# A graph layer with attention and routed experts: the last group of the middle stage in another order

## The reference

```python
deg = maximum(segment_sum(ones, dst, 6250), 1)
xn = layernorm(x)                                   # 6250 x 512
x = x + gnn(xn, src, dst, deg) + attention(xn)      # 100000 edges, 8 heads, linear attention
t = layernorm(x)
shared = sum over 2 of  gelu(t @ sw1.T + sb1) @ sw2.T + sb2
probs = softmax(t @ gate_w.T + gate_b)              # 8 experts, the two best of each row
routed = sum over the two best e of  probs[e] * (gelu(t @ rw1[e].T + rb1[e]) @ rw2[e].T + rb2[e])
out = x + shared + routed
```

## Time and profile before

| what | value |
|---|---|
| median of 3 runs | 2157.23 us (2155.22 to 2158.01) |
| the profiled execution | 2157.89 us |
| its span | 2156.3 us |
| its granted TensorE clock | 0.979 of full |
| TensorE busy over the span | 2012.7 us (93%) |
| VectorE busy | 1524.0 us (71%) |
| ScalarE busy | 1070.1 us (50%) |
| GpSimd busy | 1274.1 us (59%) |
| the stretch of the change | 1472.8 to 1519.8 us |

### The profile page before, as it was taken

One profiled execution on the slowest core, in us unless ns is written; L12 is line 12 of the kernel. 1 busy time (PEld: TensorE's weight loads), 2 busy tenths in 40 slices (PEclk: granted clock), 3 DMA queues, 4 the chain that ended last, 5 costly groups with the idle time before them and its releaser, 6 DMA issues. The chain is left out here.

```text
span 2156.3 us, 47156 instructions
## 1 busy us (share of the span) xinstructions
PE 2012.7 (93%) x12724; PEld 1356.5 (63%) x12725; DVE 1524.0 (71%) x3774; ACT 1070.1 (50%) x2102; POOL 1274.1 (59%) x1360
## 2 busy tenths in 40 slices
PE   5999997999999999999999999995799999889998
PEld 2555554666666666666666666663577777667776
DVE  7888885668887787877888787886344444356666
ACT  3555774645546565565645555452344444323332
POOL 3666776777777777777777777760233333153442
PEclk9999998999999999999999999997799999999999
DMA  8855646788888888888888888874455555567765
GB/s 294 271 163 171 247 163 174 226 257 265 261 266 270 259 255 259 264 256 258 256 260 268 252 258 259 262 236 166 146 166 175 170 167 170 165 218 259 256 241 203
DMA packets 187677, 492.47 MB, mean 228 GB/s; under 512 B 41357, under 2 KB 54157, under 8 KB 185833
## 3 DMA queue, kind: packets, MB, share of 16 engines
q0 software_dynamic: 91920, 306.84, 47.0%
q1 hardware_dynamic: 65929, 135.51, 18.1%
q10 hardware_dynamic: 29775, 49.51, 6.7%
HBM read 371.29 MB, written 120.41 MB: 228 GB/s over the span
## 5 line engine op out<-in xcount | busy, mean ns | idle before, releaser
L692 POOL DMA_INDIRECT region<-table,idx x112 | 110.2, 984 | 289.6 <-DMA region<-table,idx 203.9
L642 POOL DMA_INDIRECT region<-table,ebuf x225 | 216.5, 962 | 78.4 <-issue 78.1
L642 POOL DMA_INDIRECT Wff<-table,ebuf x225 | 215.5, 958 | 75.3 <-issue 68.3
L347 PE MATMUL bank<-Wff,region 128*125 128x512 f16 (+2 forms) x620 | 238.7, 385 | 13.4 <-DVE region L2132 7.5
L653 POOL DMA_INDIRECT Wff<-table,ebuf x200 | 210.1, 1050 | 60.9 <-issue 60.9
L348 PE MATMUL bank<-Wff,region 128*125 128x512 f16 (+2 forms) x620 | 237.4, 383 | 0.0
L349 PE MATMUL bank<-Wff,region 128*125 128x512 f16 (+2 forms) x620 | 237.2, 383 | 0.0
L653 POOL DMA_INDIRECT region<-table,ebuf x200 | 198.6, 993 | 61.0 <-issue 60.4
L1189 PE MATMUL bank<-region,ohs 128*125 128x512 f16 x850 | 190.8, 382 | 5.2 <-DMA region<-table,ebuf 5.2
L1189 PE MATMUL bank<-Wff 128*125 128x512 f16 x850 | 191.5, 384 | 0.4 <-DMA Wff<-table,ebuf 0.4
L871 ACT ACTIVATE region<-bank,dg 125x512 f32<-125x512 f32 x50 | 34.4, 687 | 271.7 <-DVE counted L1794 211.3
(11 more groups left out here) (328 smaller groups left out, 5461.9 us busy)
## 6 DMA issues: line engine op xcount, KB each, us to landing
yd<-region ACTq DMA_DIRECT2D x55, 512.0 KB
x2d<-region SPq DMA_DIRECT2D x25, 512.0 KB
table<-region SPq DMA_DIRECT2D x25, 512.0 KB, 4.4
region<-x2d SPq DMA_DIRECT2D x25, 512.0 KB, 5.0
table<-region POOLq DMA_DIRECT2D x50, 250.0 KB, 3.7
xnt<-region POOLq DMA_DIRECT2D x25, 500.0 KB, 4.0
region<-xnt SPq DMA_DIRECT2D x25, 500.0 KB, 4.5
x2t<-region SPq DMA_DIRECT2D x25, 500.0 KB
```

Of the source, the lines that this page charges most:

```text
L347: wmm(ps, xh, wh, start=first, stop=False)
L642: pool.indirect_dma_start(out=ring[j][:, s, :], out_offset=None, in_=table, in_offset=bass.IndirectOffsetOnAxis(ap=ebuf[j][:, 2 * s:2 * s ...
L692: pool.indirect_dma_start(out=tg[:, turn, c, :], out_offset=None, in_=table2, in_offset=bass.IndirectOffsetOnAxis(ap=idx[:, 2 * turn + c:2 ...
```

## The change

It touches the last group of the middle stage and the first step of the expert stage, on all five engines. The gate of group NG - 2 leaves `group(NG - 1)` on VectorE and ScalarE. VectorE does it behind the bias of group NG - 1 and ahead of the split, ScalarE behind the casts. TensorE's places of NG - 2 go behind the attention matmuls. For the last group, the statistics of the first tile of x2 come between the two x2, and ScalarE normalises and casts tile by tile. Both list operands of NG - 2 come ahead of the last gate on VectorE, and the first of its list matmuls ahead of the last gate matmuls on TensorE. GpSimd reads the first step's list where VectorE wrote it, without the DMA into `idx`; the counts of `ix_in` go down by one.

```diff
@@ sync
             store_x2(NG - 1)
             store_normalised(NG - 1)
-            sp.wait_ge(sem["idx_set"], 2)
-            sp.dma_start(idx[:, 0:2], idx_all[:, 0:2]).then_inc(sem["ix_in"], 16)
             sp.wait_ge(sem["agg_end"], NT)
@@ gpsimd, rows_of
+                    listed = idx[:, 2 * turn + c:2 * turn + c + 1] if past(r) else idx_all[:, c:c + 1]
                     pool.indirect_dma_start(
                         out=tg[:, turn, c, :], out_offset=None, in_=table2,
-                        in_offset=bass.IndirectOffsetOnAxis(ap=idx[:, 2 * turn + c:2 * turn + c + 1].bitcast(U32), axis=0),
+                        in_offset=bass.IndirectOffsetOnAxis(ap=listed.bitcast(U32), axis=0),
                     ).then_inc(sem["g_in"], 16)
 
-            pool.wait_ge(sem["ix_in"], 16)
+            pool.wait_ge(sem["idx_set"], 2)
             pool.nop().then_inc(sem["ix_taken"], 1)
             rows_of(0, 0)
             pool.wait_ge(sem["sched2_set"], 1)
             total = pool.value_load(sched2[0:1, NE:NE + 1], min_val=NE + 1, max_val=400)
-            pool.wait_ge(sem["ix_in"], 32)
+            pool.wait_ge(sem["ix_in"], 16)
...
-                    list_in = pool.to_reg((r + 1) * 16)
+                    list_in = pool.to_reg(r * 16)
@@ scalar (normalised and split_normalised take the tiles to do as an argument)
-                if prev is not None:
+                if prev is not None and nxt is not None:
                     gate(prev)
...
-                normalised(i)
+                if nxt is not None:
+                    normalised(i)
...
             group(NG - 1, NG - 2, None, None)
-            split_normalised(NG - 1)
+            for j in range(G):
+                normalised(NG - 1, (j,))
+                split_normalised(NG - 1, (j,))
+            gate(NG - 2)
             turned(NG - 1)
             gate(NG - 1)
@@ tensor
                 if nxt is not None:
                     aggregate(nxt, 0, first)
-                if prev is not None:
-                    places(prev)
+                    if prev is not None:
+                        places(prev)
...
             group(NG - 1, NG - 2, None)
+            places(NG - 2)
             turn_normalised(NG - 1)
+            slot_list(NG - 2, 0)
             pe.wait_ge(sem["gate_dve"], GATE_STEPS * (NG - 2) + 13)
             gate(NG - 1)
-            slot_list(NG - 2, 0)
             slot_list(NG - 2, 1)
             places(NG - 1)
@@ vector
                 moments(i, sem["h_step"], 1.0, 0)
-                if prev is not None:
+                if prev is not None and nxt is not None:
                     gate(prev)
...
                     stt(x2[:, j, :], bank[j][0:T, :], sv[0:T, S_ATT:S_ATT + 1], hh[:, j, :], ALU.mult, ALU.add).then_inc(sem["x2_sb"], 1)
-                for j in range(G):
-                    row_stats(i, j, x2[:, j, :], sem["x2_sb"], sem["z_step"])
+                    if nxt is None:
+                        row_stats(i, j, x2[:, j, :], sem["x2_sb"], sem["z_step"])
+                if nxt is not None:
+                    for j in range(G):
+                        row_stats(i, j, x2[:, j, :], sem["x2_sb"], sem["z_step"])
...
-                if prev is not None:
+                if prev is not None and nxt is not None:
                     places(prev)
...
             group(NG - 1, NG - 2, None)
+            gate(NG - 2)
             split_normalised(NG - 1)
+            places(NG - 2)
             listed(NG - 2, 0)
+            listed(NG - 2, 1)
             gate(NG - 1)
-            listed(NG - 2, 1)
             places(NG - 1)
```

More of the change, by code:

```diff
@@ L881, in _, with normalised @@
             act.wait_ge(sem["mh_done"], 1)
-            def normalised(i):
-                for j in range(G):
+            def normalised(i, tiles=range(G)):
+                for j in tiles:
                     act.wait_ge(sem["z_step"], (NORM_STEPS + 1) * (i + 1))
@@ L888, in normalised, with split_normalised @@
                     act.activation(bank[j][0:T, :], x2[:, j, :], ACT.Identity, scale=rs[:, j, :], bias=nm[:, j, :]).then_inc(sem["tn_sb"], 1)
-            def split_normalised(i):
-                for j in range(G):
+            def split_normalised(i, tiles=range(G)):
+                for j in tiles:
                     act.wait_ge(sem["tn_sb"], 2 * i + j + 1)
```

## The result

The kernel after takes 2150.41 us (median of 10 runs, 2148.12 to 2152.57), the kernel before 2155.41 in the 10 runs beside it (2154.84 to 2160.48). The ratio is 0.9972, with an interval of 0.9963 to 0.9982: faster by 0.28%, 4 to 8 us. In a second comparison the changed kernel took 2150.07 (5 runs, 2146.5 to 2152.15) against 2155.94 (15 runs, 2153.22 to 2159.41), ratio 0.9964 [0.9951, 0.9978]. The forecast was 2152.4, so it is 2.0 too high; the time lies inside the range given.

What follows compares the result with a forecast made beforehand. A chain of hand-offs at the end of the middle stage was taken as the bound, its gain passing on nearly whole. 3.05 plus 1.8 made 4.85 us, giving a median of 2152.4 us, range 2149.8 to 2155.6.

Steps and rivals of the forecast that it cites:

- The level: Whole kernel: profiled execution lies 0.66 us above the median of 2157.23, so its 2153.0 after the change means median 2152.4.
- The sum: End of the middle stage to the expert stage's first transposes: 3.05 plus 1.8 makes 4.85 us gained.
- Gate off the path ahead of attention: VectorE ahead of the last group's attention matmuls: moving the gate of NG-2 away starts them 2.84 us earlier.
- The clock: TensorE's 24 attention matmuls: no change in slow ones; none slow would gain about 1.3 us, all slow lose 3.2.
- Early statistics: VectorE, last group: only the second tile's statistics stay behind the second x2, gain 0.45 us.
- The gate's new place: VectorE behind the bias: reciprocal waits for ScalarE's exponentials, costing 1.87 us, so 1.42 of 3.29 is left at the split.
- tile by tile casts: ScalarE, last group: each cast waits for the op directly ahead of it, priced at 0.15 us in all.
- Lists ahead: TensorE and VectorE, last gate: gate matmuls 0.8 us later than possible, yet places at 1501.42 instead of 1504.47.
- List in place: GpSimd's first gather: the list DMA's 1.78 us falls out, gain 1.8 us, bounds 0 and 2.76.
- The clock didn't hold: Rival, attention matmuls: clock stays up under them, 1.3 us more won, total gain 6.2, 2151.1 us; chance 0.14.
- The tail: Rival, end of last group: ScalarE hand-offs or exponentials cost more, total gain only 3.2 us, 2154.0; chance 0.18.
- the slower rival: Expert stage's first steps: TensorE stays at 1.2 GHz two steps more, up to 12 us, giving 2164; chance 0.04.

Runs made afterwards that it cites:

- the two experiments on the kernel before: Kernel before with only the first list gathered in place (2932.38 us, ratio 0.999), and with only the first tile's statistics between the two x2 (2930.85 us, 0.9994).
- filler: Changed kernel plus 16 useless matmuls where TensorE idles ahead of the last group's attention matmuls: 2149.3 us, ratio 0.996.
- the experiment: Changed kernel with ScalarE's old order for the last group, both tiles normalised, then both cast: 2956.95 us, ratio 0.9979.

## Why the prediction was right and where it was not

**The level.** This is the step that failed: "it lies 0.66 above the median of 2157.23, so the median goes to 2152.4". The three runs shown (2155.22, 2157.23 and 2158.01) are the first of the ten runs of the same kernel beside the changed one, and their median is 1.8 us above that of all ten, 2155.41 (those of the second comparison: 2155.94, and 2155.7 by itself). Of the 2.0 us by which 2152.4 is too high, 1.8 is this and 0.2 is the gain. Beside the kernel before as it then ran, 2152.4 stands for a gain of only 3.0 us, half of the 6.0 that the ratio shows, though the working had 4.85. The chances didn't suffer from it: the bound for faster would move from 2152.9 to 2151.1 and the forecast to 2150.6, and the 0.5 us between them stays. The three runs went from 2155.22 to 2158.01; I treated their middle as the kernel's time to a tenth of a percent, though even one execution of before that was profiled later took 2152.05, 3.7 below its median. In the two profiled executions of the kernel before, all of the difference is made ahead of the change: the reference stands at 1473.30 and 1467.55, 5.8 us apart with the same code, and the spans differ by 5.8 too. In those of after it stands at 1470.98 and 1469.20.

**The sum.** 4.85 was forecast for the first transposes; the first pair shows 4.76 and all pairs 3.6 to 4.8. The medians are 5.0 apart. The ratio, which weighs the runs side by side, says 6.0 with an interval of 4 to 8, and the second comparison 7.8 with 4.7 to 10.6 (its medians are 5.9 apart). So the times show 1.2 us and more beyond the rows, and the smallest pair of the rows lies outside both intervals. No trace has the rest: the reference stands at 1467.55 and 1473.30 in before and at 1469.20 to 1471.63 in the four executions of changed kernels that take 2150 us, and from the first transposes to the end of the span are 636.5 and 636.7 us in before and 636.1 and 636.7 in after. It stays open; 4.85 is confirmed by the rows, and by the times only in that it lies inside both intervals.

- *Gate off the path ahead of attention:* 2.85, forecast 2.84.
- *The clock:* taken as no change, with bounds of -1.3 and +3.2. From the attention's start to the second x2 it is 7.37 and 7.14 in before, 7.69 and 8.41 in after: 0.3 to 1.3 lost, inside the bounds. It isn't a thing of the change: in the two experiments on the kernel before in which attention starts at 6.04 and 6.03, the same distance is 8.19 and 8.35, as long as in after. With the same start, 7 to 14 of the 24 matmuls were slow in the kernels that start at 3.19 without filler, and they ended 10.24 to 11.50 behind the reference. This term makes most of the spread of the 3.6 to 4.8, the landing of the gathered rows the rest (0.2).
- *Early statistics:* 0.45 forecast, 0.46 to 0.52 measured.
- *The gate's new place:* the split 4.10 behind the bias by my working, 4.15 in the rows. The tile by tile casts: 0.15 forecast, 0.2 by the experiment.
- *Lists ahead:* the gate matmuls 4.69 behind the split, measured 4.64; the places 2.84 behind VectorE's gate, measured 2.85; the worth of this part by itself 1.7.
- *List in place:* 1.8 at the gather, measured 1.8, there and at the transposes.
- *Behind it:* from the first to the last transposes 352.4 in both executions of before, 352.9 and 352.8 in after. The gain passes on nearly whole.

**The rivals.** The clock didn't hold; the mechanism is real, as the filler shows, but the change leaves TensorE idle 3.71 us, as the prediction had it. The prediction counted the rule of the Trainium skill (page TensorE: Matmul & The Clock Gate, section Why this matters for your kernels) for this rival; for a gap of that length the rule speaks against it, and so does the trace. The price of 1.3 was near: the filler gave 1.5 from where the sum had that x2. The tail costs what was forecast, and the list's DMA was last. The expert stage starts at its clock as before: its first five steps begin 0, 9.71, 16.63, 24.00 and 30.21 us behind the first transposes in before and 0, 9.47, 16.37, 24.76 and 30.97 in after (24.01 and 23.87 for the fourth in the second executions). The two steps at 1.2 GHz that the slower rival needed don't show.

## What to carry to other kernels

Bookkeeping that is moved off one wait must go into another engine's wait and not just somewhere later: behind the bias the gate gave back 1.7 of the 2.85 us, because its last ops need an engine that is then busy, while under the attention matmuls it cost between nothing and 0.9. Price a hand-off by the distance between two rows that have it; those terms came out within 0.1 us here, also on chips where the program is a third longer. The level is another matter: a median of three runs was off by as much as a third of the effect, so the gain should be forecast and judged apart from it, and two traces should be compared from an instruction just ahead of the change.

## What the runs showed of the hardware

The same kernel takes 2155 us on one chip and 2934 and 2965 on two others. The page of the kernel with the list in place alone, on the second chip (section of the costliest groups: busy us and mean ns, idle before and what ended it), and a stretch of its middle loop (windows, columns as above):

```profile
L1188 PE MATMUL bank<-region,ohs 128*125 128x512 f16 x850 | 294.0, 481 | 304.2 <-issue 302.9
```

```profile
550.00:2250.00 1700.00, 1199.70 (x5731) 709.49 (x5731) 793.48 (x2471) 558.16 (x1269) 706.74 (x741) 0.78 0.49 149
```

The same loop of the kernel before on the first chip:

```profile
410.00:1470.00 1060.00, 1026.24 (x6067) 694.03 (x6067) 831.50 (x2615) 590.53 (x1348) 790.83 (x806) 1.00 0.84 259
```

DMA moves 149 GB/s instead of 259, TensorE idles in front of the matmuls that take the gathered rows (304 us ahead of L1188 alone; the profile names no releaser, only "issue", but in the kernel these matmuls wait for the gathers), a group takes 76 to 78 us instead of 44.4, and the granted clock falls to 0.78 of full. A VectorE instruction takes 0.32 us in the mean and a ScalarE instruction 0.44 in both loops, and behind the loop the distances are the same. Two plain causes fall by the same rows. The DMA engines aren't slower while they are busy: 149 GB/s at a busy share of 0.49 and 259 at 0.84 are both about 305 GB/s for a share of 1. And GpSimd doesn't take longer to issue a gather (0.96 us there, 0.95 to 1.05 on the first chip), but stands idle for up to 20.5 us ahead of a tile's gathers, where on the first chip it idles 0.9 at most. By exclusion something between issue and arrival takes longer; no run here shows that directly, nor what it is.

The second surprise is the scatter of the clock under one burst: the same 24 matmuls, behind the same 3.7 us of idleness, had between 7 and 14 slow ones from one execution to the next (10 and 14 in the two of after), worth up to 1.3 us. So a change of a microsecond in such a place can't be read from one execution.
